# The mixer's change of unit in another order: low parts of the output weights behind y, ScalarE's first convolution tap ahead of their high parts

## The reference

```python
proj = input_states @ in_proj_w.T                 # gate, xBC, dt
xBC  = silu(causal_conv4(xBC) + conv_b)           # 4 taps along time, per channel
hs, Bm, Cm = split(xBC)                           # 128 heads x 64, 8 groups x 128 states
...
y_intra = (C B^T * decay * dt) @ x                # within a chunk
y_inter = (C * exp(cum)) @ previous state         # from the chunks before
y = y_intra + y_inter + D * x
g = y * silu(gate)
g = g * rsqrt(mean over the group's 1024 channels of g*g + eps) * norm_w
return g @ out_w.T
```

## Time and profile before

| what | value |
|---|---|
| time, median of 3 runs (lowest, highest) | 2132.67 us (2129.69, 2134.03) |
| time of the profiled execution | 2127.0 us |
| its span, first to last instruction | 2125.0 us |
| TensorE busy | 1984.3 us, 93% |
| VectorE busy | 1671.7 us, 79% |
| ScalarE busy | 1441.9 us, 68% |
| GpSimd busy | 1283.2 us, 60% |
| mean granted TensorE clock | 0.979 |

### The profile page before, as it was taken

How to read it: one execution, slowest core, us unless ns; L and a number is a source line. 1 busy time by engine, 2 the same in 40 slices (tenths; PEclk the granted TensorE clock), 3 DMA queues, 4 the chain that set the end, 5 groups by cost and what they waited for, 6 DMA issues and landing times.

```text
span 2125.0 us, 34073 instructions
## 1 busy us (share of the span) xinstructions
PE 1984.3 (93%) x11288; PEld 1533.7 (72%) x11288; DVE 1671.7 (79%) x3231; ACT 1441.9 (68%) x2755; POOL 1283.2 (60%) x1185
## 2 busy tenths in 40 slices
PE   8899997799999999999999999999999999999878
PEld 4666665587777777777777777777777777777665
DVE  4777665578897888888878887888788878888876
ACT  1566623677778777777787778787778787777721
POOL 4455230266777676767675767585667676766561
PEclk9999998899999999999999999999999999999989
DMA  4000010333223323232323232222222332222201
GB/s 169 2 0 0 0 56 5 95 113 104 76 78 101 114 65 97 88 112 68 109 74 116 64 105 99 85 85 89 95 89 81 94 104 90 80 90 80 85 29 40
DMA packets 125707, 166.04 MB, mean 78 GB/s; under 512 B 37777, under 2 KB 88977, under 8 KB 121330
## 3 DMA queue, kind: packets, MB, share of 16 engines
q1 hardware_dynamic: 125554, 164.11, 24.0%
HBM read 159.88 MB, written 4.20 MB: 77 GB/s over the span
## 4 chain that ended last, share of the span: by engine, by line
PE 39%; DVE 21%; ACT 19%; issue 6%; POOL 2%; SPq 0%; DMA 0%; ACTq 0%; POOLq 0%; DVEq 0%
DVE conv L807 11%; PE p_out L102 10%; PE p_mix L102 9%; PE p_gate_intra L102 7%; ACT wq_t L1773 4%; DVE w_out L1898 3%; PE p_gate_intra L1688 3%; ACT L1773 3%; PE p_inter_state L1664 3%; ACT L1783 3%; PE p_inter_state L1677 2%; ACT conv L785 2%; PE pM L102 2%; ACT x_and_gate L1783 1%; PE p_flip L1582 1%
## 5 line engine op out<-in xcount | busy, mean ns | idle before, releaser
L2108 POOL TENSOR_TENSOR wq_t<-wq_t,cb 128x1024 f32<-128x1024 f32 x128 | 316.4, 2472 | 224.2 <-ACT wq_t L1773 188.8
L102 PE MATMUL p_out<-w_out,yT 128*128 128x512 f32 x1536 | 386.7, 402 | 26.9 <-DVE attn L1936 13.8
L102 PEld LDWEIGHTS p_out<-w_out,yT 128*128 128x128 f32 x1536 | 295.1, 193 | 98.3 <-DVE yT L1918 17.3
L807 DVE SCALAR_TENSOR_TENSOR conv<-p_mix,unit_small,conv 128x511 f32<-128x511 f32 (+2 forms) x384 | 286.8, 747 | 98.7 <-ACT conv L785 87.2
L102 PE MATMUL p_gate_intra<-x_high,w_gate 128*128 128x512 f32 x1024 | 350.0, 403 | 5.9 <-POOL w_gate L2091 3.4
L102 PE MATMUL p_mix<-x_high,w_x 128*128 128x512 f32 x1024 | 351.4, 405 | 1.4 <-DVE x_low L1148 1.4
L1773 ACT ACTIVATE wq_t<-wq_t,minus_cum 128x128 f32<-128x128 f32 x1024 | 326.0, 390 | 1.4
L795 ACT ACTIVATE x_and_gate<-conv 128x512 f32<-128x512 f32 x128 | 80.8, 631 | 271.3 <-DVE conv L807 271.1
L102 PEld LDWEIGHTS p_gate_intra<-x_high,w_gate 128*128 128x128 f32 x1024 | 193.4, 189 | 44.6 <-POOL w_gate L2091 3.7
L102 PEld LDWEIGHTS p_mix<-x_high,w_x 128*128 128x128 f32 x1024 | 193.8, 189 | 39.8 <-DVE x_low L1148 1.8
L2149 POOL TENSOR_TENSOR x_to_state<-x_tokens,group_dt_end 128x512 f32<-128x512 f32 x96 | 120.9, 1259 | 156.9 <-ACT x_tokens L1730 156.9
(11 more groups left out here) (242 smaller groups left out, 4404.9 us busy)
## 6 DMA issues: line engine op xcount, KB each, us to landing
cum_all<-cum_rows SPq DMA_DIRECT2D x128, 512.0 KB, 3.8
exp_cum<-exp_rows SPq DMA_DIRECT2D x192, 128.0 KB, 3.2
w_staged<-in_w_gate SPq DMA_DIRECT2D x16, 1024.0 KB, 5.4
w_raw_tiles<-in_w_x SPq DMA_DIRECT2D x64, 256.0 KB, 3.0
w_staged<-in_w_out SPq DMA_DIRECT2D x16, 1024.0 KB, 4.9
w_raw_tiles<-in_w_bc SPq DMA_DIRECT2D x16, 256.0 KB, 5.4
x<-in_x SPq DMA_DIRECT2D x1, 2048.0 KB, 18.6
out<-x_and_gate SPq DMA_DIRECT2D x8, 256.0 KB, 2.0
```

The costliest lines, as they stand in the source:

```text
L102: last = pe.matmul(dst, left[a](k), right[b](k), start=k == 0 and n_ == 0, stop=stop and k == tiles - 1 and n_ == 2)
L807: m = dve.scalar_tensor_tensor(self.conv[:, par, back:], self.p_mix[:, bank, 0:SEQ - back], w[:, TAPS - 1 - back:TAPS - back], self.conv[: ...
L2108: pool.tensor_tensor(decay[:, k % 2], decay[:, k % 2], cb[:, c].unsqueeze(1).to_broadcast([P, UNIT_HEADS, P]), ALU.mult).then_inc(decay_do ...
```

## The change

It touches the order of instructions on three engines, and neither TensorE's nor SyncE's. No instruction is added or taken away, except that eight exponentials stand in one run where there were two runs of four.

- Step 7 and step 15, VectorE: `y_low_part` of the own step stands right behind `make_y`, ahead of the taps, instead of at the next step's head. In step 15 `out_halves` of step 14 stands ahead of `make_y`, instead of in step 0.
- Step 7, ScalarE: all eight exponentials of step 8 stand ahead of `high_y` (at step 15 still four, `high_y`, four).
- Steps 0 and 8, VectorE: the order skip part, low parts of the output weights, all taps, state, y becomes skip part, first taps, state, y, `mean_square` of the step before, remaining taps (the B/C convolution, only k = 0), low parts of the output weights.
- Steps 0 and 8, ScalarE: the first tap of the first convolution stands ahead of `out_high_part`, and `empty_x` of the next step ahead of the second `activate`.
- Steps 4, 8 and 12, GpSimd: `decayed` stands behind `to_state` and `to_scores` at k = 4 and 12; at k = 8 and 0 it stays ahead of them. ScalarE's `empty_x` at k = 4 and 12 moves ahead of the second four exponentials.

```diff
@@ ScalarE @@
                             empty_x(g, k)
+                            first_tap(convs[0][0], *convs[0][1])
                             if before:
                                 act.wait_ge(out_done, s)
                                 out_high_part(g * 2 + half, half)
-                            for i, e in convs:
+                            for i, e in convs[1:]:
                                 first_tap(i, *e)
...
                         high_y(*before)
-                        decay_exps(s, k, UNIT_HEADS // 2)
                         if c == CPS:
                             empty_x(g, k)
+                        decay_exps(s, k, UNIT_HEADS // 2)
...
-                                decay_exps(s + 1, (k + 1) % STEPS, 0, UNIT_HEADS // 2)
+                                first_part = UNIT_HEADS // 2 if half else UNIT_HEADS
+                                decay_exps(s + 1, (k + 1) % STEPS, 0, first_part)
                                 high_y(g, k)
-                                decay_exps(s + 1, (k + 1) % STEPS, UNIT_HEADS // 2)
+                                decay_exps(s + 1, (k + 1) % STEPS, first_part)
@@ VectorE @@
-                        if c == 0 and before:
-                            y_low_part(*before)
-                        if older:
+                        if older and c != 1:
                             mean_square(*older)
-                        if older and older[1] >= CHUNKS:
+                        if older and older[1] >= CHUNKS and k:
                             out_halves(*older)
...
+                        convs = [(i, e) for i, e in enumerate(events) if e[0][0] != "cb"]
+                        if c == CHUNKS - 1:
+                            if half and not last:
+                                out_halves(*before)
+                            make_y(g, k)
+                            if not (last and half):
+                                y_low_part(g, k)
+                            taps_of(convs)
...
+                        if c == 0 and before:
+                            taps_of(convs[:1])
+                            keep_state()
+                            make_y(g, k)
+                            mean_square(*before)
+                            taps_of(convs[1:])
+                            out_low_part(g * 2 + half, half, 0, UT)
+                            continue
@@ GpSimd @@
-                        if c % CPS == 0:
+                        if c == 0:
                             decayed(g, k)
                         pool.wait_ge(flip_out, s + 1)
...
-                        if c % CPS:
+                        if c:
                             decayed(g, k)
```

More of the change, by code:

```diff
@@ L1774, in decay_exps @@
                                            bias=neg[:, s // STEPS % 2, c, head:head + 1])
-                    if hi == UNIT_HEADS:
+                    if lo < hi == UNIT_HEADS:
                         m.then_inc(exp_done, 1)
@@ L1831, in group @@
                                 keep_half(*before)
+                            if before:
+                                empty_x(g, k + 1)
                             for i, (e, _, index) in convs[1:]:
@@ L1836, in group @@
                                 silu_gate(s)
-                            empty_x(g, k + 1)
+                                empty_x(g, k + 1)
                             continue
@@ L1891, in _, with out_low_part @@
                 dve.memset(one[:], 1.0).then_inc(const3, 1)
-                def out_low_part(unit, half):
-                    for j in range(UT):
+                def out_low_part(unit, half, lo, hi):
+                    for j in range(lo, hi):
                         at_ = UT * (TAPS + 1) + j
@@ L2003, in group @@
                             arguments(s + 1, k + 1)
-                        if c and before:
+                        if c:
                             y_low_part(*before)
@@ L2030, in taps_of @@
                         def taps_of(events):
-                            for i, (e, fill, index) in enumerate(events):
+                            for i, (e, fill, index) in events:
                                 if e[0] != "cb":
@@ L2034, in taps_of, with keep_state @@
                                                    1 - half if c >= CPS else half)
-                        if c == CHUNKS - 1:
-                            make_y(g, k)
-                            taps_of(events)
-                            if last and half:
-                                ahead_norm(k)
-                            continue
-                        if c == 0 and not (first and k == 0):
-                            out_low_part(g * 2 + half, half)
-                        taps_of(events)
-                        if 3 <= c < 3 + UT and not (last and half):
-                            front.x_high_part(dve, g * 5 + 4 + 3 * half + (c - 3) // 2, c - 3)
-                        if first and k == 0:
-                            out_low_part(0, 0)
-                        if feeds(c):
+                        def keep_state():
                             nf = n_feeds(g, k)
@@ L2058, in group @@
                                 dve.tensor_copy(flat, p_state[:]).then_inc(state_done, 1)
+                        convs = [(i, e) for i, e in enumerate(events) if e[0][0] != "cb"]
[6 more added lines that the diff above has]
+                            taps_of(convs)
+                            if last and half:
+                                ahead_norm(k)
+                            continue
[6 more added lines that the diff above has]
+                            out_low_part(g * 2 + half, half, 0, UT)
+                            continue
+                        taps_of(convs)
+                        if 3 <= c < 3 + UT and not (last and half):
+                            front.x_high_part(dve, g * 5 + 4 + 3 * half + (c - 3) // 2, c - 3)
+                        if c == 0:
+                            out_low_part(0, 0, 0, UT)
+                        if feeds(c):
+                            keep_state()
                         make_y(g, k)
```

## The result

The changed kernel is slower: 2137.63 us median of 20 runs (2130.06 to 2147.28) against 2129.76 (2127.19 to 2134.34) for the kernel before, also 20 runs. The ratio is 1.0036, 95% interval [1.0024, 1.0048]. I had forecast 2119 in a range of 2112 to 2132. That was 13.5 us off the 2132.7 of three runs; off the 2129.8 of these 20 it would have been 2116.

A forecast was written before the change was run, and what follows sets the result against it. TensorE, 93% busy, was taken to bind, with a VectorE-ScalarE chain just behind. Terms: -11.4 + 1.6 + 0.7 - 6.3 + 3.2 - 1.3 = -13.5 us, from 2132.7 to 2119; range 2112 to 2132.

The forecast's parts named there:

- p15: Start of step 15's output product, which runs in the step behind: at 1023.97 instead of 1025.93, counted as 2.1 us.
- p7: Start of step 7's output product: 1.45 us earlier in groups 1 to 7, 1.3 in group 0, together -11.4 us.
- y8: End of low y of step 8: 0.2 us later against p7, eight times, +1.6 us.
- y0: End of low y of step 0: 0.1 us later per group, +0.7 us, with a new 2.6 us wait of TensorE.
- Step 4: Earlier end of decayed lets the intra product start 0.9 us earlier; a gain of TensorE alone, nothing on the chain.
- Clock: Four slow stretches behind the 1.96 us wait go, -6.3 us; new ones behind the wait at step 8's product, +3.2.
- Tail: Last group, step 12: VectorE's wait for inv_rms behind decayed goes, intra product binds about 1.3 us earlier: -1.3 us.
- A: Rival: low parts at 4.4 us hold back low y of steps 0 and 8: +19 us, 2138; chance 0.17.
- B: Rival: slow clock follows each wait at step 8's product, those at step 0 half covered: +12, 2131; chance 0.14.
- C: Rival: chain through steps 1 to 7 later by 1 us, p7 gains 0.4, not 1.45: +7, 2126; chance 0.14.

The follow-up runs named there:

- e3_table_early: Changed kernel plus a one-column Silu on ScalarE ahead of its wait for the late taps: 2112.9 us, 0.9915 of the kernel before.
- e1_taps_before_y: Changed kernel with VectorE's taps ahead of low y again in steps 7 and 15: 2134.1 us, 1.0019 of the kernel before.
- b3_table_early_only: Kernel before with only the one-column Silu put ahead of ScalarE's wait for the late taps: 2131.4 us, ratio 1.0010.
- b2_y_first_only: Kernel before with only VectorE's moves in steps 7 and 15 (low y right behind y, output halves ahead): 2126.7 us, ratio 0.9989.
- e7_skip_ahead: Changed kernel with the one-column Silu, plus the skip part of steps 4 and 12 ahead of low y: 2113.4 us, 0.9923 of the kernel before.
- e2: Changed kernel with GpSimd's decayed and ScalarE's empty_x of steps 4 and 12 as before: 2133.4 us, 1.0012 of the kernel before.
- e5: Changed kernel with the one-column Silu added and the edit of steps 4 and 12 taken back: 2121.8 us, 0.9968 of the kernel before.

## Why the prediction was wrong

**The step that failed** is the claim under *p15* and *p7* that low y could go ahead of the taps with nothing behind them late ("both are done before TensorE is free"), and with it under *y8* that the first tap "is bound by TensorE's projection, about 0.15 earlier". The prediction named what low y waits for and not what is queued behind the taps. Behind y the taps end 3.58 us later at step 15 and 4.29 at step 7 (1129.42 - 1125.13), where it was 2.22 before (1125.64 - 1123.42), since they now stand behind low y and behind its wait for ScalarE's high y; behind them ScalarE waits, with a table load of 1.28 us that is behind the wait too; behind that the transposes, the projection, the first tap and the chain to y8. The first tap ended 7.05 us after p7 by the forecast and 8.46 in the trace (1134.94 + 0.78 - 1127.26). This is missing in the sum eight times with 1.24 us (104.41 - 103.17) and seven times with 1.15: **+18**. That it is the load and the place of low y together is shown from four sides: without the load the cost goes (e3_table_early), with the taps first it goes too and another wait comes (e1_taps_before_y), in the kernel before the same edit gains nothing (b3_table_early_only), and with low y first alone the wait of the transposes is there, 0.6 us in the mean (b2_y_first_only).

The Trainium skill ("ScalarE: Activation LUTs", section What ACT_TABLE_LOAD costs) gives 1283 ns for the load, which the trace's 1.28 confirms, and 1380 ns of draining with it, which does not show here: the activation began 0.02 us behind the load.

The other terms:

- *y0*: right. p15 to y0 was to be 18.5 + 2.1 + 0.1 = 20.7; it was 20.71 once the load was early, and the low parts took the 2.73 us forecast. The wait of step 1 was 2.39 for 2.6.
- *Step 4*: the mechanism was right for TensorE (the wait is gone) and wrong in "on the chain nothing changes there". Moving `decayed` back put GpSimd's tokens beside VectorE's skip part, which took 5.09 us for 0.86. The taps began 0.94 us behind the first tap's end, and y0 to p7 is 0.44 to 0.52 us longer. The term of -11.4 thus came out at -8.3 over the eight groups: **+3**.
- *p7*: -1.05 us in place of -1.45. Without step 4's edit it was 80.12 - 81.60 = -1.48, and high y of step 7 came 0.03 us behind y in place of 0.77. So the term was right and the difference is the one above.
- *y8*: without the load p7 to y8 was 17.41, 0.27 later than the 16.94 + 0.2 forecast; the low parts took 4.16 us for 3.5. **+2** in eight groups.
- *p15*: y8 to p15 was to be 88.74 - 2.1 = 86.64; without a stretch at 0.50 it was 85.76, 0.88 better, **-6** in the seven groups that another follows. The starts of the output products in e3_table_early show where: 0.34 us at step 8, whose product begins 0.10 behind low y in place of 0.44, and 0.31 and 0.33 at steps 12 and 14, where the kernel before has small waits for `mean_square` (0.15 and 0.23 us). The prediction had the first and some 0.45 of the others, but set them against the clock.
- *Clock*: the four old stretches went (-6.3, as said), and five came behind the waits of step 9 at about 1.05 us each, +5 for the +3.2 forecast; five more at step 1 cost nothing, as forecast (y0 to p7 80.52 and 80.53 us in the two groups without one, 80.54 to 80.59 in four of the five with one). That is the profiled execution, at a clock of 0.975; the median of the runs has 0.971, and more stretches there may be a part of the 4.8 us between the two forms of the result (3.1 and 7.9). They need not be all of it: at a clock of 0.970 the spans of the changed kernel reach from 2136.0 to 2145.3 us, so something beside the clock varies too. Late arguments at step 9 could be another part; no run of this kernel that was profiled has them.
- *Tail*: from y0 of the last group to the end after is 1.5 us shorter, with 1.3 us of the load's cost in it; what is left, with the other terms above taken out, is **-1**.

In sum: -13.5 + 18 + 3 + 2 - 6 + 2 - 1 = +4.5. From the mixer's first y0 on, the profiled execution of after is 5.0 us longer (its span 3.0, and its first y0 at 422.3 in place of 424.3).

Of the rivals, A had the right result (2138) mostly for a reason that did not occur: the low parts took 2.73 at step 0, and at step 8, where they took 4.16, they cost 0.27 and not 0.9. B was half right, at step 9 only. C had the right place, steps 1 to 7, but its lateness was 0.4 us, from GpSimd at step 4 and not from ScalarE at step 7. Had the load been seen, the sum would have been +4.5, or 2137; that this is the measured time is in part luck, since the other errors (+3, +2, -6, +2, -1) cancel; the edit to make alongside was the one-column Silu, for 2113.

**Left open:** why the clock falls behind a wait of 1.87 us in most groups of e7_skip_ahead and few of e3_table_early, where the waits and what surrounds them are the same. A wait's length does not tell how many stretches follow, and they decide up to some 12 us here (12 stretches fewer at 1.05). And why, of VectorE's arguments and GpSimd's `decayed`, which begin together, now one and now the other takes long.

## What to carry to other kernels

When work moves ahead of something on an in-order engine, follow the thing that is put back, over every engine that waits for it, until it meets slack; look there for the instructions a compiler has placed (table loads), which the source does not show and which wait with the instruction they serve. If an engine stands idle before such a load, a one-column activation of the same function ahead of the wait takes it into the idle time, for 0.20 us. And where two kernels differ by less than the slow stretches of the clock cost, compare lengths within the trace as well as the medians; they may have different signs. Look there too whether one instruction has two durations, before the difference is put down to the clock.

## What the runs showed of the hardware

- A load of ScalarE's table does not begin while its activation waits for another engine: 2.54 us idle, then 1.28 us of load. Placed early it is worth 18 us of the lengths in this kernel and 24.8 in the medians, and nothing in the one before.
- VectorE's small instructions with all operands in SBUF end one for one with GpSimd's beside them: 5.09 us for work of 0.86. Where two long ones began 0.04 to 0.05 us apart, either could be the one drawn out: VectorE's took 1.21 us and GpSimd's 3.5, or 3.37 and 2.34, in 11 of the 24 groups of e1, e2 and e5. The output weights' low parts, also from SBUF, took 2.73 us without GpSimd and 4.16 beside `x_to_state` and `x_dt`, while taps that read PSUM kept their 2.30 to 2.32 us.
- The same wait of TensorE, 1.87 us in the same place, was followed by 3.4 us at a clock of 0.50 (1.2 GHz) in six of eight groups of e7_skip_ahead, in two of e3_table_early and in one when that ran again. Waits of 0.7 to 1.7 us were followed by none in any kernel up to 130 us behind the last y0, and the eleven of 4.0 us all were (e1, e2, e5).
